# Attention turns of two key tiles on one Trainium2 core: the subtraction of the row maxima as one round of four 32-row tiles, the two products with V back to back

## The reference, cut to what matters

```python
qkv = X @ W_qkv + b_qkv
Q, K, V = split per head            # 16 heads, 64 wide each
scores = einsum('bhqd,bhkd->bhqk', Q, K) / sqrt(64)
attn = softmax(scores, axis=-1)
out = einsum('bhqk,bhkv->bhqv', attn, V)
return out.reshape(b, l, 16 * 64) @ W_fc + b_fc
```

## Time and profile before

| what | value |
|---|---|
| median of 3 runs | 1833.4 us (1829.42 to 1833.78) |
| the profiled execution's own time | 1829.79 us |
| its span, first to last instruction | 1827.8 us |
| TensorE busy | 1730.8 us, 95% |
| VectorE, ScalarE, GpSimd busy | 1300.0, 853.0, 1133.2 us |
| granted clock of TensorE, mean | 0.975 |

### The profile page before, as it was taken

One profiled execution on the slowest core, in us unless ns is written; L12 is line 12 of the kernel. 1 busy time (PEld: TensorE's weight loads), 2 busy tenths in 40 slices (PEclk: granted clock), 3 DMA queues, 4 the chain that ended last, 5 costly groups with the idle time before them and its releaser, 6 DMA issues. The chain is left out here.

```text
span 1827.8 us, 29321 instructions
## 1 busy us (share of the span) xinstructions
PE 1730.8 (95%) x9675; PEld 874.4 (48%) x9675; DVE 1300.0 (71%) x2175; ACT 853.0 (47%) x1176; POOL 1133.2 (62%) x517
## 2 busy tenths in 40 slices
PE   4899999999999999999999999999999999845996
PEld 3444444444444444444444444444444444334886
DVE  5677766767777766667777776766767776487887
ACT  3344444444444444444444444444444444325874
POOL 3376666666677666676676776666666677620134
PEclk8899999999999999999999999999999999958999
DMA  2000000000000000000000000000000001000010
GB/s 88 18 13 18 18 18 17 17 17 17 17 17 17 17 17 17 17 12 11 17 13 16 17 17 17 17 17 17 17 17 17 17 18 48 1 23 24 30 35 29
DMA packets 31039, 37.07 MB, mean 20 GB/s; under 512 B 2173, under 2 KB 25242, under 8 KB 31002
## 3 DMA queue, kind: packets, MB, share of 16 engines
q1 hardware_dynamic: 30848, 36.58, 5.9%
q10 hardware_dynamic: 154, 0.03, 0.0%
HBM read 14.58 MB, written 2.10 MB: 9 GB/s over the span
## 5 line engine op out<-in xcount | busy, mean ns | idle before, releaser
L519 POOL TENSOR_TENSOR ACC<-ACC,PR 128x1024 f32<-128x1024 f32 x382 | 909.0, 2380 | 194.8 <-ACT PR L566 177.8
L566 ACT ACTIVATE PR<-ps_s 128x1024 f32<-128x1024 f32 x512 | 524.0, 1023 | 742.3 <-PE ps_s L758 742.3
L593 DVE TENSOR_REDUCE NMH<-ps_mx 128x2 f32<-128x1024 f32 x508 | 620.3, 1221 | 305.1 <-PE ps_mx L739 300.8
L768 PE MATMUL ps_o<-PR,V 128*64 128x512 f32 x2048 | 552.1, 617 | 0.0
L519 POOL TENSOR_TENSOR ACC<-PR 128x1024 f32<-128x1024 f32 x64 | 152.2, 2378 | 293.8 <-ACT PR L566 293.8
L624 DVE RECIPROCAL SUM<-SUM 128x128 f32<-128x128 f32 x256 | 241.3, 945 | 86.0 <-ACT SUM L549 86.0
L752 PEld LDWEIGHTS ps_s<-QH,KH 64*128 64x128 f32 x1024 | 95.6, 183 | 416.6 <-issue 250.1
L752 PE MATMUL ps_s<-QH,KH 64*128 64x512 f32 x1024 | 256.6, 497 | 1.2 <-ACT PR L566 1.2
L739 PE MATMUL ps_mx<-KH,QH 64*128 64x512 f32 x1016 | 202.7, 394 | 4.4 <-DVE NMH L593 4.4
L754 PE MATMUL ps_s<-QL,KH 64*128 64x512 f32 x1024 | 203.3, 392 | 0.0
L756 PE MATMUL ps_s<-QH,KL 64*128 64x512 f32 x1024 | 202.6, 392 | 0.0
(11 more groups left out here) (189 smaller groups left out, 1638.9 us busy)
## 6 DMA issues: line engine op xcount, KB each, us to landing
hcur<-hT SPq DMA_DIRECT2D x32, 512.0 KB, 2.9
Wraw<-in_L_attn_W_qkv SPq DMA_DIRECT2D x32, 192.0 KB, 2.4
x<-in_L_attn_X SPq DMA_DIRECT2D x4, 512.0 KB, 5.2
Wfc<-in_L_attn_W_fc SPq DMA_DIRECT2D x32, 64.0 KB, 1.8
hT<-in_L_attn_X SPq DMA_DIRECT2D x4, 512.0 KB, 6.0
out<-e_res SPq DMA_DIRECT2D x7, 256.0 KB, 2.3
e_hTs<-hT_hi SPq DMA_DIRECT2D x6, 256.0 KB, 2.7
e_hTs<-hT_lo SPq DMA_DIRECT2D x6, 256.0 KB, 3.2
```

What stands on the lines that cost most here:

```text
L519: G.tensor_tensor(ACC[:, ch, :, :], a, PR[:, t, :, :], ALU.add).then_inc(added, 1)
L566: A.activation(PR[:, t, :, :], ps_s[:, :, :], ACT.Exp, scale=SCALE).then_inc(exp_done, 1)
L593: D.tensor_reduce(NMH[:, ch, :, i, kc], banks[:, :, :], AX, ALU.max, negate=True).then_inc(mx_red, 1)
L768: last = T.matmul(ps_o[half(h), ch, :], V[:, u, t, half(h)], PR[:, t, h, :], start=(t == 0), stop=(t == 7))
```

## The change

A pair is now eight turns of two steps. `ps_s` has four banks, two for each of the turn's steps; `ps_o` has one bank and `ps_w` one, so PSUM is still eight banks. In a turn TensorE does: a round of maxima; the three rounds of scores of the first step and of the second; `minus_max`, which adds the negated maxima to all four banks in one round of four matmuls of 32 rows each; the second round of maxima; a unit of the table `FULL` (128-row matmuls); the two products with V of the turn before; a unit of the table `SPLIT` ("sums" and "rows", both now in matmuls of 64 columns like the products with V). `QM` therefore holds the maxima in four 32-row quarters instead of two halves, `NM` gets them twice (two small reductions on VectorE), and "rows" is two plain matmuls with the identity instead of a transpose. ScalarE is released by `scored` for both exponentials at once, reads the units after them, and copies `ps_o` to `O` once per chunk (`copy_o`); VectorE multiplies `O` in place. The first chunk of K of a pair is now projected two pairs ahead (`k, 2, 0` in turn 6), so `first` also prepares K of pair 1, and three instead of two maxima.

```diff
-        ps_s = psum("ps_s", [P, 2, 512])
+        ps_s = psum("ps_s", [P, 4, 512])
         ps_mx = psum("ps_mx", [P, 2, 512])
-        ps_o = psum("ps_o", [P, 2, 512])
-        ps_w2 = psum("ps_w2", [P, 2, 512])
+        ps_o = psum("ps_o", [P, 512])[:, :]
+        ps_w = psum("ps_w", [P, 512])[:, :]
...
+        EARLY = 3
+        FULL = {0: ("k", 1, 1), 1: ("q", 1, 0), 2: ("v", 1, 0), 3: ("fc", -1, 1),
+                4: ("q", 1, 1), 5: ("v", 1, 1), 6: ("k", 2, 0), 7: ("fc", 0, 0)}
+        SPLIT = {0: ("sums", -1, 1), 2: ("rows", 0, 1), 4: ("sums", 0, 0), 6: ("rows", 1, 0)}
+        INVERT_A = {1: (-1, 1, 0), 2: (-1, 1, 2), 5: (0, 0, 0), 6: (0, 0, 2)}
+        INVERT_B = {1: (-1, 1, 1), 2: (-1, 1, 3), 5: (0, 0, 1), 6: (0, 0, 3)}
...
+            def copy_o(n, ch):
+                act.wait_ge(pv_done, 16 * n + 8 * ch + 8)
+                wait(act, fc_mm, 2 * n + ch)
+                A.activation(O[:, :], ps_o[:, :], ACT.Copy).then_inc(o_copied, 1)
...
             def pair(n, u):
+                for j in range(8):
+                    for s in (2 * j, 2 * j + 1):
...
+                        A.activation(PR[:, t, :, :], ps_s[:, half_s:half_s + 2, :], ACT.Exp, scale=SCALE).then_inc(exp_done, 1)
+                    x = unit_at(FULL, n, j)
+                    if x and x[0] != "fc":
+                        unit(x[0], x[1], unit_u(FULL, j, u), x[2], ps_w)
+                    if j == 0 and has(n - 1):
+                        copy_o(n - 1, 1)
+                    if j == 4:
+                        copy_o(n, 0)
+                    x = unit_at(SPLIT, n, j)
+                    if x and x[0] != "rows":
+                        unit(x[0], x[1], unit_u(SPLIT, j, u), x[2], ps_w)
...
-                    dve.wait_ge(pv_done, 16 * m + 8 * ch + 8)
-                    wait(dve, fc_mm, 2 * m + ch)
-                    D.tensor_tensor(O[:, :], ps_o[:, ch, :], SUM[:, :], ALU.mult).then_inc(o_norm, 1)
+                    dve.wait_ge(o_copied, 2 * m + ch + 1)
+                    D.tensor_tensor(O[:, :], O[:, :], SUM[:, :], ALU.mult).then_inc(o_norm, 1)
...
             def pair(n, u):
+                for j in range(8):
+                    for s in (2 * j, 2 * j + 1):
+                        d, ch, i, kc = place(s)
+                        if has(n + d):
+                            reduce_max(n + d, ch, i, kc, 16 * n + s + EARLY + 9)
+                        if s % 2 == 0 and j in INVERT_A and has(n + INVERT_A[j][0]):
+                            invert(n + INVERT_A[j][0], *INVERT_A[j][1:])
+                    x = unit_at(FULL, n, j)
                     if x:
+                        unit(x[0], x[1], unit_u(FULL, j, u), x[2], ps_w)
+                    if j in INVERT_B and has(n + INVERT_B[j][0]):
+                        invert(n + INVERT_B[j][0], *INVERT_B[j][1:])
+                    x = unit_at(SPLIT, n, j)
+                    if x:
+                        unit(x[0], x[1], unit_u(SPLIT, j, u), x[2], ps_w)
...
                 elif kind == "rows":
-                    T.transpose(ps_w[:, 0:P], flat(NM[:, ch, :, :]), g.ident[:, :]).then_inc(rows_t, 1)
+                    for h in range(2):
+                        last = T.matmul(ps_w[half(h), 0:P], NM[:, ch, h, :], g.ident[:, :], start=True, stop=True)
+                    last.then_inc(rows_t, 1)
...
-                for h in range(2):
-                    last = T.matmul(ps_s[:, h, :], ONE[half(h), :], QM[half(h), u, q], start=False, stop=True)
-                last.then_inc(scored, 1)
+            def minus_max(u, s):
+                ch = s // 8
+                q = slice(ch * 512, ch * 512 + 512)
+                for r in range(4):
+                    h, v = divmod(r, 2)
+                    last = T.matmul(ps_s[:, 2 * v + h, :], ONE[quarter(r), :], QM[quarter(r), u, q], start=False, stop=True)
+                last.then_inc(scored, 2)
...
+            def next_unit(table, n, u, j):
+                x = unit_at(table, n, j)
+                if x:
+                    ahead = unit_ahead_of(table, n, j)
+                    if ahead:
+                        freed(*ahead)
+                    if x[0] == "rows":
+                        pe.wait_ge(mx_both, 2 * x[1] + x[2] + 1)
+                    unit(x[0], x[1], unit_u(table, j, u), x[2], ps_w)
+
             def pair(n, u):
+                for j in range(8):
+                    next_maxima(n, u, 2 * j)
+                    scores(n, u, 2 * j)
+                    scores(n, u, 2 * j + 1)
+                    minus_max(u, 2 * j)
+                    next_maxima(n, u, 2 * j + 1)
+                    next_unit(FULL, n, u, j)
+                    v_of_last_steps(n, u, j)
+                    next_unit(SPLIT, n, u, j)
```

More of the change, by code:

```diff
@@ L554, in first @@
                     if kind != "rows":
-                        unit(kind, 0, 0, ch, ps_w2[:, k % 2, :])
-                split_w(1, 1)
+                        unit(kind, m, m, ch, first_bank(k))
             def pair(n, u):
[L559 to L570, removed]
+                for j in range(8):
+                    for s in (2 * j, 2 * j + 1):
+                        ch, t = divmod(s, 8)
+                        chunk = 2 * n + ch
+                        wait(act, pv_done, 16 * n + s - 7)
+                        wait(act, added, 7 * (chunk - 1) + max(t, 1))
+                        act.wait_ge(scored, 16 * n + s + 1)
+                        half_s = 2 * (s % 2)
+                        A.activation(PR[:, t, :, :], ps_s[:, half_s:half_s + 2, :], ACT.Exp, scale=SCALE).then_inc(exp_done, 1)
[9 more added lines that the diff above has]
+                        unit(x[0], x[1], unit_u(SPLIT, j, u), x[2], ps_w)
+                    if j == 5 and has(n + 2):
@@ L641, in first @@
-                for i in range(2):
+                    reduce_max(0, 0, i // 2, i % 2, i + 1, first_max_banks(i))
+                dve.wait_ge(s_mask, 5)
+                unit("rows", 0, 0, 0, first_bank(6))
+                split_w(1, 1)
+                unit("k", 1, 1, 0, first_bank(7))
+                for i in range(EARLY):
                     reduce_max(0, 1, i // 2, i % 2, i + 9)
-                split_w(1, 1)
             def pair(n, u):
[L646 to L650, removed]
-                    if x:
[L652 to L656, removed]
+                for j in range(8):
[6 more added lines that the diff above has]
+                    x = unit_at(FULL, n, j)
+                    if x:
+                        unit(x[0], x[1], unit_u(FULL, j, u), x[2], ps_w)
[4 more added lines that the diff above has]
+                        unit(x[0], x[1], unit_u(SPLIT, j, u), x[2], ps_w)
+                    if j == 5 and has(n + 2):
@@ L764, in times_v @@
                 if t == 0:
[L765 removed]
+                    wait(pe, o_copied, 2 * n + ch)
                     pe.wait_ge(v_copied, 2 * n + 2)
                 for h in range(2):
[L768 removed]
+                    last = T.matmul(ps_o[half(h), :], V[:, u, t, half(h)], PR[:, t, h, :], start=(t == 0), stop=(t == 7))
                 last.then_inc(pv_done, 1)
@@ L790, in v_of_last_step, with v_of_last_steps @@
+            def v_of_last_steps(n, u, j):
+                if j > 0:
+                    times_v(n, u, 2 * j - 2)
+                    times_v(n, u, 2 * j - 1)
                 elif has(n - 1):
+                    times_v(n - 1, 1 - u, 14)
                     times_v(n - 1, 1 - u, 15)
-            def pair(n, u):
-                for s in range(16):
-                    d, ch, i, kc = place(s)
-                    scores(n, u, s)
-                    if has(n + d):
-                        maxima(n + d, u if d == 0 else 1 - u, ch, i, kc, 16 * n + s + 10)
-                    x = unit_at(n, s)
-                    if x and x[0] == "sums":
-                        v_of_last_step(n, u, s)
-                    if x:
-                        k = ORDER.index(s) - 2
-                        before = unit_at(n, ORDER[k]) if k >= 0 else has(n - 1) and unit_at(n - 1, ORDER[k])
-                        if before:
-                            freed(*before)
-                        if x[0] == "rows":
-                            pe.wait_ge(mx_both, 2 * x[1] + x[2] + 1)
-                        unit(x[0], x[1], unit_u(s, u), x[2], ps_w2[:, ORDER.index(s) % 2, :])
-                    if not x or x[0] != "sums":
-                        v_of_last_step(n, u, s)
```

113 lines of the change are left out of this document (65 added, 48 removed).

## The result

The changed kernel takes 1944.36 us (median of 4 runs, 1933.58 to 1946.63), the kernel before beside it 1833.59: a ratio of 1.060, 95% interval 1.059 to 1.062. The forecast was 1851 with a range to 1878. It is slower, as forecast, but by 111 us instead of 18.

The account below looks back on a forecast made before the run. TensorE's list was taken to bound the kernel. Per pair -1.4 own time and +2.0 waits gave +0.6, 17.4 over 29 pairs; with +7.2 at the start and -4.7 at the end, +19.9: 1851 us, range 1802 to 1878.

Parts of the forecast that it names:

- What bounds it: In the attention, TensorE's list sets the pair's 48.0 us; it is busy for all but 1.6 of 1527 us.
- TensorE's own time: Per pair, rounds gain 1.8, shape changes stay at 7.9, "rows" costs 0.17 more, twice: -1.5, or -1.4 with rounding.
- B (shapes free, faster): Rival, 11%: going between 64 and 32 rows on TensorE costs nothing; 42 us under the forecast, 1809.
- C (two by two): Rival, 13%: the four 32-row matmuls go two by two, 0.46 a round; 46 us more, 1897.
- The start: Before pair 0, extra K projection and maxima chain: first scores at about 71 instead of 63.86, +7.2 us.
- Waits ahead of "sums" and "rows": In turns 0, 4 and 6 TensorE waits for VectorE's read of a projection: about 0.4 each, 1.2 per pair.
- the prediction's terms without turn 7: Per pair: TensorE's own change of -1.4 and the three waits of 1.2, on the 48.0 before.
- Rival D: 8%: waits half or less because ScalarE or VectorE overlap more; 1820, with no waits about 1790.
- Costed at nothing: Items priced at zero: output copies on ScalarE, the product from another memory, second small reduction, GpSimd's additions, SyncE's queue.
- The wait of turn 7: TensorE waits 0.7 to 0.8 before turn 7's second maxima, because VectorE comes late out of turn 6.

Follow-up runs that it names:

- e1: Changed kernel with GpSimd's additions cut to 8 columns, leaving out the sums of the exponentials: 1847.71 us, ratio 1.009.
- e2: Changed kernel with the product with the reciprocals moved from VectorE to GpSimd's own list, nothing left out: 1849.14 us, ratio 1.009.
- e4: Kernel before, with only the output copied to SBUF by ScalarE and multiplied there by VectorE: 1853.09 us, ratio 1.011.
- e9: Changed kernel with each GpSimd addition issued as two halves of 512 columns: 1892.56 us, ratio 1.034.
- e10: e2 with the 32-row round replaced by two rounds of two 64-row matmuls in the same place: 1830.11 us, ratio 0.999.
- e6: e2 with each step's negated maxima added by its own two 64-row matmuls, releasing ScalarE per step: 1752.61 us, ratio 0.957.
- e8: e1 with an idle VectorE instruction of 1.76 us ahead of the product of turn 6: 1962.67 us, ratio 1.070.

## Why the prediction was right and wrong

**What bounds it, and TensorE's own time: right.** Round, shapes, V and units came out as priced: 0.23 for the round, side by side, 0.44 with its shapes, and full price for going between 64 and 32 rows. Rivals B (shapes free, faster) and C (two by two) fall; e1 shows the sum of those terms, 1847.7 against 1851. The start was mis-sized by little: the first scores come at 73.57, not 71.

**Waits ahead of "sums" and "rows": right**, 0.45 in the turn shown, 0.4 forecast. e2, which has these and no wait in turn 7, has pairs of 47.9; the prediction's terms without turn 7 give 48.0 - 1.4 + 1.2 = 47.8. Rival D falls with that.

**The step that failed** stands under "Costed at nothing": "The product with the reciprocals is the same instruction from another memory." With `ps_o` as its operand it took 0.69 beside any addition; with `O` in SBUF it takes up to 2.38, since it is held until GpSimd's addition ends (e1, e4, e9). The prediction gave this cost no bounds, though the trace of the kernel before has rows for it: among the instructions of `gate_rows` in pair 1 is one of the product's width whose operands lie in SBUF and which meets an addition, and one like the product without an addition beside it. Timeline of GpSimd and VectorE before:

```profile
123.58 2.38 POOL L519 TENSOR_TENSOR ACC<-ACC,PR 128x1024 f32<-128x1024 f32 x1 [0.85 <-ACT PR L566]
124.91 1.60 DVE L667 SCALAR_TENSOR_TENSOR mod_rep<-mod_rep 128x512 f32<-128x512 f32 x1
...
137.48 0.68 DVE L675 TENSOR_TENSOR mod_rep<-mod_rep,on_rep 128x512 f32<-128x512 f32 x1
```

The first ends at 126.51, 0.55 behind the addition (125.96); in e1, where no addition is beside it, it takes 0.68. By these rows a product that meets the whole of an addition could have been priced at up to 2.38 + 0.55 = 2.9 instead of 0.69. The Trainium skill (SBUF — State Buffer, "SBUF: two separate sides") states the rule for such a hold: VectorE instructions with two SBUF inputs and GpSimd instructions that read SBUF share a pair of ports, and whichever starts first has it for its whole instruction. The trace agrees: 0.55 from the addition's end to the product's in both the kernel after and e9, and in e9 GpSimd held in turn (1.73 for 1.29).

**The wait of turn 7** was the right wait at the right place with the wrong size, 2.3 for 0.7, since the product stands ahead of it on VectorE's list. The product of turn 6 is 1.67 longer (2.36 for 0.69), and turn 7 goes from e1's 6.29 to 7.98, 1.69 more.

**The fall of the clock inside the attention was not in the prediction.** After 2.3 us idle it fell to 1.2 GHz in about every other pair, 1.57 us each time (9.55 - 7.98), and twice for about 3. With a wait of 1.3 (e9) or 0.7 (e1) it did not fall once.

Summed, from the two profiled executions: 1943.7 less e1's 1844.3 is 99. Turn 7 of pairs 2 to 29 holds 77 of them, 28 times 1.69 for the lateness (47) and 30 for the clock. Pairs 0 and 1 hold 9; in pair 1 the instructions of `gate_rows` are held too. Turn 3 is 0.15 longer in each pair (4), and the start, the last two pairs and what follows them hold the other 9. All of it goes with the additions (e1), but by which step these last 13 do is not shown, and what decides in which pairs the clock falls stays open.

## What to carry to other kernels

Moving an operand of a VectorE instruction from PSUM to SBUF is not free beside a GpSimd that adds in SBUF: look what GpSimd does at that moment, and what stands behind the instruction on VectorE's list. "The same instruction from another memory" is a new price: look in the trace for a row with operands in that memory beside the same neighbour, even if it runs only once. Such an instruction goes onto GpSimd's own list, to a place where GpSimd adds nothing (95 us back, e2), or the additions are cut shorter (52 us back, e9). Packing small rounds into one with smaller tiles pays only if the changes of shape (here 0.21 to go in and the same to come out) cost less than the round saved (0.23). And a round for two steps keeps back the engine behind it: with one for each step, and nothing else changed, the time went from 0.999 (e10) to 0.957 (e6) of that before.

## What the runs showed of the hardware

A product of 0.69 us took up to 2.38 beside GpSimd's additions with both operands in SBUF, and 0.69 with one of them in PSUM. The hold is for one instruction at a time, either way round: a half addition went from 1.29 to 1.73. Two operands in SBUF are not the only case: a TENSOR_SCALAR of `gate_rows`, which reads one tensor in SBUF and writes it there, took 2.21 in the changed kernel, 1.11 before and 0.36 in e1, and ended 0.28 to 0.29 behind the addition where it met one. The reciprocals (0.94), which also read and write SBUF, were not held. And an engine that is only late can cost more than its lateness: waits of 2.3 us were followed by the half clock in many pairs (after: 18 stretches, e8: 29), waits of 1.3 in none.
